# Windowed attention and FFN, six layers: value products with two stationaries per head pair, and another order of the work on five engines

## The reference, cut to what matters

```python
for i in range(6):
    x = attn_layer(shift_tokens(x), Wqkv[i], q_scale[i], k_scale[i], Wo[i]) + x
    x = ffn_layer(shift_tokens(x), ln_g[i], ln_b[i], W1[i], b1[i], W2[i], b2[i]) + x

# attn_layer: 16 heads of 64, windows of 32 tokens
q = l2norm(q) * qs;  k = l2norm(k) * ksc        # then rotary tables with a decay
sim = einsum('bhwie,bhwje->bhwij', bq, bk2) * 8 # 32 queries, 64 keys: window before + own
attn = softmax(where(mask, -max, sim));  out = einsum('bhwij,bhwje->bhwie', attn, bv2)
# ffn_layer: layernorm, x @ W1 + b1, a * gelu(gate), @ W2 + b2 (inner 341)
```

## Time and profile before

| | |
|---|---|
| median of 3 runs | 3135.85 us (3133.73 to 3137.84) |
| profiled execution | 3140.72 us, span 3138.9 us |
| mean granted TensorE clock | 0.989 of full speed (2.4 GHz) |
| PE, PEld busy | 97%, 70% |
| DVE, ACT, POOL busy | 96%, 86%, 81% |

### The profile page before, as it was taken

One profiled execution on the slowest core, in us unless ns is written; L12 is line 12 of the kernel. 1 busy time (PEld: TensorE's weight loads), 2 busy tenths in 40 slices (PEclk: granted clock), 3 DMA queues, 4 the chain that ended last, 5 costly groups with the idle time before them and its releaser, 6 DMA issues.

```text
span 3138.9 us, 168648 instructions
## 1 busy us (share of the span) xinstructions
PE 3047.6 (97%) x71268; PEld 2184.2 (70%) x71268; DVE 3011.6 (96%) x5981; ACT 2692.7 (86%) x5251; POOL 2554.7 (81%) x2803
## 2 busy tenths in 40 slices
PE   6997999999999999999999999999999999999996
PEld 3553777777777777777777777777777777777775
DVE  6997999999999999999999999999999999999995
ACT  5995888888888888888888888888888888888885
POOL 6986888888888888888888888888888888888883
PEclk8998999999999999999999999999999999999998
DMA  3001222223222223222223222223222223222221
GB/s 83 10 10 30 57 52 59 56 52 89 62 52 62 53 52 91 60 54 61 53 56 88 59 58 57 52 60 86 57 62 53 52 62 89 52 62 53 55 60 52
DMA packets 151240, 182.27 MB, mean 58 GB/s; under 512 B 51668, under 2 KB 74258, under 8 KB 151186
## 3 DMA queue, kind: packets, MB, share of 16 engines
q1 hardware_dynamic: 151186, 181.55, 22.3%
HBM read 21.32 MB, written 2.10 MB: 7 GB/s over the span
## 4 chain that ended last, share of the span: by engine, by line
PE 91%; POOL 3%; issue 2%; ACT 2%; DVE 1%; SPq 1%; DMA 0%; POOLq 0%; ACTq 0%; DVEq 0%
PE bank L1518 11%; PE bank L1475 9%; PE bank L1444 8%; PE bank L1546 7%; PE bank L1453 6%; PE bank L1563 5%; PE bank L1408 5%; PE bank L1528 5%; PE bank L1487 5%; PE bank L1554 5%; PE bank L1495 5%; PE bank L1508 5%; PE bank L1501 4%; PE bank L1422 4%; PE bank L1436 2%
## 5 line engine op out<-in xcount | busy, mean ns | idle before, releaser
L1167 DVE TENSOR_REDUCE sm<-sq 128x32 f32<-128x2048 f32 x192 | 437.0, 2276 | 0.0
L1518 PEld LDWEIGHTS bank<-wo,oT 128*128 128x128 f32 x3072 | 372.9, 192 | 91.7 <-issue 90.1
L1518 PE MATMUL bank<-wo,oT 128*128 128x128 f32 x3072 | 374.2, 275 | 0.8 <-ACT gl L839 0.8
L580 POOL TENSOR_TENSOR qk<-qk,rn 128x512 f32<-128x512 f32 x192 | 200.1, 1042 | 213.2 <-DVE rn L1124 213.2
L1475 PEld LDWEIGHTS bank<-PT,vs 64*64 64x64 f32 x18432 | 288.9, 135 | 94.5 <-issue 93.8
L625 POOL TENSOR_TENSOR P<-P,rowsum 128x512 f32<-128x512 f32 x192 | 200.1, 1042 | 154.4 <-DVE rowsum L1202 154.3
L1475 PE MATMUL bank<-PT,vs 64*64 64x32 f32 (+1 forms) x18432 | 311.0, 220 | 4.2 <-issue 4.2
L1546 PEld LDWEIGHTS bank<-cst,qk 32*128 32x128 f32 x12288 | 206.7, 137 | 147.5 <-issue 147.2
L1444 PEld LDWEIGHTS bank<-qkT 64*32 64x32 f32 x24576 | 279.1, 105 | 15.9 <-issue 5.7
L1444 PE MATMUL bank<-qkT 64*32 64x64 f32 x24576 | 282.6, 225 | 4.6 <-issue 4.6
L637 POOL TENSOR_TENSOR qk<-ta,tb 128x512 f32<-128x512 f32 x192 | 245.5, 1279 | 5.8 <-DVE tb L1212 5.8
(11 more groups left out here) (177 smaller groups left out, 9365.5 us busy)
## 6 DMA issues: line engine op xcount, KB each, us to landing
vs<-vt SPq DMA_DIRECT2D x1152, 128.0 KB, 2.4
wqkv<-L_ffn_Wqkv SPq DMA_DIRECT2D x18, 512.0 KB, 3.7
zm<-zm SPq DMA_DIRECT2D x192, 31.8 KB
wo<-L_ffn_Wo SPq DMA_DIRECT2D x6, 512.0 KB, 4.9
z_sb<-x SPq DMA_DIRECT2D x4, 512.0 KB, 6.1
ctxb<-ctx SPq DMA_DIRECT2D x32, 64.0 KB, 1.8
w<-L_ffn_W SPq DMA_DIRECT2D x6, 341.0 KB, 3.2
out<-x_sb SPq DMA_DIRECT2D x7, 256.0 KB, 2.7
```

The lines of the kernel that those rows point to most:

```text
L1167: v_.tensor_reduce(sm[:, :], sq[:, :].rearrange("p (h d) -> p h d", d=DH), AX.X, ALU.add).then_inc(s["d_sumsq"], 1)
L1518: ins = t_.matmul(bank[7][:, 384:512], oT[:, c, :], wo[:, 2 * (c % 4) + c // 4, :], start=c == 0, stop=c == PAIRS - 1)
```

## The change

It has four parts.

1. Value products. The probabilities go to two buffers: PTA with queries 0 to 95 for tokens 0-63, and PTC with queries 64 to 127 for tokens 64-127. For queries 64 to 95, which see tokens 32 to 95, one half of the keys lies in each buffer and the other half is zero there; the copies make the zeros by a scale with a value for each partition (0 or 1). For that the keys and the mask of that window are put in swapped order in the scores. Two stationaries are left, and two DMAs for each half of the heads. The products into PTA and PTC add up in PSUM.
2. Roots. The Newton step moves: ScalarE squares the root (`a_r2`) and forms 3 - x (`a_n2`), GpSimd does the two products (`g_n1`, `g_rn`); VectorE keeps the maximum, now as a reduction over pairs. A factor 0.5 moves into the rotary constants.
3. Order. All engines get another order. TensorE's is now: z transpose, last key projection, value projection, probability transposes of n-3, mask and scores of n-2, transpose of normed z of n-5, value projection, query projection of n+1, gate and FFN of n-5, query projection of n+1, output projection of n-4, q/k transposes of n-1, key projection of n+1, second FFN product of n-5, value products of n-3 (two groups), which are the last thing in the slot. Output projection and FFN run one slot later than before (lags 4 and 5 for 3 and 4).
4. SyncE. The biases of the next layer load at its start, the weights a few steps earlier or later than before. The unrolled start has eight slots for six.

ScalarE's order is now: key square, table load for the gelu, `a_n2` of n-1, vt copy of bank 0, shifted z copy, last quarter to PTC, znT, PTA copy, vt copy of bank 1, third quarter to PTA, query square, gelu, third quarter to PTC, table load, ln, exp of the probabilities, query square, exp of the root, two q/k copies, `a_r2`, key square, two q/k copies, two output copies.

```diff
-                    for j in range(3):
-                        sp.dma_start(vs[rows, par, j, :], vt[32 * j:32 * j + 64, par, r, :]).then_inc(s[f"l_v{par}"], 16)
+                    for j in range(2):
+                        sp.dma_start(vs[rows, par, j, :], vt[64 * j:64 * j + 64, par, r, :]).then_inc(s[f"l_v{par}"], 16)
...
+                    wait(pool, "a_r2", done(u))
+                    g.tensor_tensor(n1[:, :], sc[:, :], n0[:, :], ALU.mult).then_inc(s["g_n1"], 1)
...
+                    wait(pool, "a_n2", done(u))
+                    g.tensor_tensor(rn[:, p, :], rn[:, p, :], n2[:, :], ALU.mult).then_inc(s["g_rn"], 1)
...
+                    a_.activation(n2[:, :], n1[:, :], ACT.Identity, scale=-1.0, bias=three[:, 0:1]).then_inc(s["a_n2"], 1)
...
+                    wait(act, f"l_v{p}", 64 * ((u - 2) // 2) + 64 if isinstance(u, int) else (u >> 1) * 64)
+                    wait(act, "p_v0", done(u))
+                    a_.activation(vt[:, p, 0, :], bank[0][:, :], ACT.Copy).then_inc(s["a_v0"], 1)
...
-                    a_.activation(PT[:, :, 0:64], bank[4][:, :].rearrange("p (h q) -> p h q", h=PAIRS), ACT.Copy).then_inc(s["a_PT0"], 1)
...
+                    a_.activation(PTC[:, :, 32:64], bank[5][:, :].rearrange("p (h q) -> p h q", h=PAIRS)[:, :, 32:64], ACT.Copy).then_inc(s["a_PC1"], 1)
+                    a_.activation(PTA[:, :, 0:64], bank[4][:, :].rearrange("p (h q) -> p h q", h=PAIRS), ACT.Copy).then_inc(s["a_PA0"], 1)
+                    a_.activation(PTA[:, :, 64:96], bank[5][:, :].rearrange("p (h q) -> p h q", h=PAIRS)[:, :, 0:32], ACT.Copy, scale=cst[:, C_HALF:C_HALF + 1]).then_inc(s["a_PA1"], 1)
+                    a_.activation(PTC[:, :, 0:32], bank[5][:, :].rearrange("p (h q) -> p h q", h=PAIRS)[:, :, 0:32], ACT.Copy, scale=cst[:, C_HALF + 1:C_HALF + 2]).then_inc(s["a_PC0"], 1)
...
+                    wait(act, "a_rn", done(u))
+                    a_.activation(n0[:, :], rn[:, p, :], ACT.Square).then_inc(s["a_r2"], 1)
...
-                    v_.scalar_tensor_tensor(sm[:, :], sm[:, :], NORM_MIN2, sm[:, :], ALU.max, ALU.max).then_inc(s["d_nr0"], 1)
+                    v_.tensor_reduce(sc[:, :], sm[:, :, :], AX.X, ALU.max).then_inc(s["d_nr0"], 1)
...
+                    for i in range(4):
+                        for r in range(2):
+                            for e in range(2):
+                                ins = t_.matmul(bank[4 + r][64 * e:64 * e + 64, 128 * i + 0:128 * i + 96],
+                                                vs[kr, p, 0, hc:hc + 64], PTA[kr, 4 * e + i, :],
+                                                start=i == 0, stop=False, skip_group_check=True)
+                    ins.then_inc(s["p_AV0"], 1)
...
+                                ins = t_.matmul(bank[4 + r][64 * e:64 * e + 64, 128 * i + 64:128 * i + 128],
+                                                vs[kr, p, 1, hc:hc + 64], PTC[kr, 4 * e + i, :],
+                                                start=False, stop=True, skip_group_check=True)
+                        if i % 2 == 1:
+                            ins.then_inc(s["p_AV"], 1)
```

More of the change, by code:

```diff
@@ L453, in _ @@
                     shift_v(end + 1, 1)
-                else:
+                if last:
                     store(0, 6)
@@ L458, in _ @@
                     load_o(layer + 1)
+                if not last:
                     shift_v(end + 2, 0)
-                    load_b2(layer + 1)
             store(6, 9)
@@ new lines, in slot @@
+                u, on, p = unit(n, k, -1)
+                if on:
+                    wait(act, "p_qk0", done(u))
+                    wait(act, "d_sumsq", done(u - 1))
+                    a_.activation(sq[:, 0:512], bank[0][:, :], ACT.Square, scale=LN_UP ** 0.5).then_inc(s["a_sq0"], 1)
+                u, on, p = unit(n, k, 5)
+                if on:
+                    wait(act, "p_gate", done(u))
+                    edge(act, u, "d_h", done(u - 1))
+                    for j, (_, m) in enumerate(FCH):
+                        ins = a_.activation(gl[0:m, j, :], bank[7][0:m, 128 * j:128 * j + 128], ACT.Gelu, bias=small[0:m, 5 + j:6 + j])
+                    ins.then_inc(s["a_gelu"], 1)
@@ new lines, in slot @@
+                if on:
+                    wait(act, "p_qk1", done(u))
+                    edge(act, u, "d_sumsq", done(u - 1))
+                    a_.activation(sq[:, 512:1024], bank[1][:, :], ACT.Square, scale=LN_UP ** 0.5).then_inc(s["a_sq1"], 1)
+                u, on, p = unit(n, k, 0)
+                if on:
+                    wait(act, "a_ln", done(u))
+                    edge(act, u, "g_qk0", done(u - 2))
+                    edge(act, u, "g_qk1", done(u - 2))
+                    edge(act, u, "g_qk2", done(u - 2))
+                    edge(act, u, "g_qk3", done(u - 2))
+                    a_.activation(rn[:, p, :], lns[:, :], ACT.Exp, scale=-0.5).then_inc(s["a_rn"], 1)
@@ new lines, in slot @@
+                u, on, p = unit(n, k, 0)
+                if on:
+                    wait(act, "a_rn", done(u))
+                    edge(act, u, "g_n1", done(u - 1))
+                    a_.activation(n0[:, :], rn[:, p, :], ACT.Square).then_inc(s["a_r2"], 1)
+                u, on, p = unit(n, k, -1)
+                if on:
+                    wait(act, "p_qk2", done(u))
+                    edge(act, u, "d_sumsq", done(u - 1))
+                    a_.activation(sq[:, 1024:1536], bank[0][:, :], ACT.Square, scale=LN_UP ** 0.5).then_inc(s["a_sq2"], 1)
@@ L832, in slot @@
                     a_.activation(oT[:, 0:4, :], bank[4][:, :].rearrange("p (h q) -> p h q", h=4), ACT.Copy).then_inc(s["a_AV0"], 1)
-                u, on, p = unit(n, k, 4)
-                if on:
-                    wait(act, "p_gate", done(u))
-                    edge(act, u, "d_h", done(u - 1))
-                    for j, (_, m) in enumerate(FCH):
-                        ins = a_.activation(gl[0:m, j, :], bank[7][0:m, 128 * j:128 * j + 128], ACT.Gelu, bias=small[0:m, 5 + j:6 + j])
-                    ins.then_inc(s["a_gelu"], 1)
@@ L1430, in slot @@
                     edge(pe, u, "a_tr2", done(u))
+                    edge(pe, u, "a_tr3", done(u))
                     pe.nop(nofuse=True)
@@ L1488, in slot @@
                     ins.then_inc(s["p_gate"], 1)
-                u, on, p = unit(n, k, 0)
-                if on:
-                    edge(pe, u, "a_zs", done(u))
-                    edge(pe, u, "d_rot2", done(u))
-                    wait(pe, "l_wv", 16 * layer_of(u) + 16)
-                    t_.matmul(bank[0][:, :], zsT[:, p, :], wv[:, :, 0, :], start=True, stop=True).then_inc(s["p_v0"], 1)
-                u, on, p = unit(n, k, 4)
+                u, on, p = unit(n, k, 5)
                 if on:
@@ L1547, in slot @@
                     ins.then_inc(s["p_tr"], 1)
-                u, on, p = unit(n, k, 4)
+                u, on, p = unit(n, k, -1)
                 if on:
-                    wait(pe, "d_h", done(u))
+                    wait(pe, "d_rot0", done(u))
+                    edge(pe, u, "a_zs", done(u))
+                    wait(pe, "l_wk", 16 * layer_of(u) + 16)
+                    t_.matmul(bank[0][:, :], zsT[:, p, :], wqkv[:, 1024:1536], start=True, stop=True).then_inc(s["p_qk2"], 1)
+                u, on, p = unit(n, k, 5)
+                if on:
+                    edge(pe, u, "d_h", done(u))
                     wait(pe, "l_w2", 32 * layer_of(u) + 32)
```

556 lines of the change are left out of this document (283 added, 273 removed), and 10 rows, old and new, of the table names.

## The result

The changed kernel takes 3192.82 us (median of 4 runs, 3190.42 to 3193.79) against 3135.91 of the kernel before in the same session: 1.0176 times, 95% interval 1.0163 to 1.0189. It is slower, as forecast, but the size is off: +57 us where +27 was forecast. The time lies inside the wide range (3095 to 3220) and outside the forecast's own (3135 to 3180). The span went from 3138.9 to 3191.5 us.

What follows compares the result with a forecast made beforehand. TensorE was taken as the bound, then a 14.77 us loop through the value rows' DMA landing against 14.66 before. 3135.85 + 21 (188 slots x 0.11) + 6 (drain) = 3163 us; own range 3135 to 3180, wide 3095 to 3220.

Steps and rivals of the forecast that it cites:

- Value products at 1.3 us: TensorE's 64 value-product pairs, 32 of 96 and 32 of 64 columns, take 1.3 us a slot against 1.53 before.
- Rival B: Each quadrant loads and streams one after the other: value products stay at 1.5 to 1.6, 3200 to 3219 us; chance 0.20.
- The landing: Value rows' DMAs, issued 0.13 us after the value products, land at 4.25; ScalarE's vt copy waits 0.9 us.
- Rival A: The DMA landing doesn't bind and the slot is TensorE's 14.43 us: 3099 us; chance 0.31.
- ScalarE's row from the copy to the gelu's end: ScalarE's pieces from the vt copy through the gelu take 4.34 us, so the gelu ends at 8.59.
- it starts at 8.64: TensorE's output projection, waiting for the gelu that ends at 8.59, starts at 8.64 us after the z transpose.
- 188 equal slots: About 188 of 192 slots are steady, each losing 0.11 us: +21 us.
- Projection that waited, 1.99: An output projection that waited takes 1.99 us to the next tiled group, 0.1 more, its first load being exposed.
- Drain +6: In the drain the last value products come behind gate, FFN and output products: 6 us, bounds 0 and 14.5.
- TensorE alone 14.43: TensorE's own slot without the landing wait: 13.13 of other work plus 1.3 of value products, 14.43 us.
- Roots at nothing: Moving the root's steps from VectorE to ScalarE and GpSimd buys nothing by itself; their added work is covered.
- Rival C: ScalarE becomes the bound, its scaled and tiny copies taking full duration: 15.2 us a slot, 3243 us; chance 0.05.

Runs made afterwards that it cites:

- e7: e1 with each 96-column value product issued as 64 + 32 columns with the same stationary, 96 pairs for 64; 3200.41 us, ratio 1.0204.
- e1: Changed kernel with ScalarE's last-quarter copy to PTC and half copy to PTA moved ahead of the vt copy that waits for the DMAs; 3137.58 us, ratio 1.001.
- e3: Changed kernel with the four DMAs of value rows moving 256 of 512 columns, so the result isn't the reference's; 3127.47 us, ratio 0.9974.
- e10: Changed kernel with zsT and last-quarter copy ahead of ScalarE's waiting vt copy, register-valued waits of both projections first, TensorE's loop body rotated; 3078.17 us, ratio 0.9816.
- e2: Changed kernel with the two waits ahead of TensorE's output projection swapped: weights' semaphore first, then the gelu's; 3184.52 us, ratio 1.0158.
- e8: e1 with the root's small GpSimd product and ScalarE three-minus step each issued once more into unread buffers; 3157.41 us, ratio 1.0071.
- e11: e10 without the rotation of TensorE's loop body, so the value products end it again; 3093.78 us, ratio 0.9865.
- e9: e1 with TensorE's loop body rotated, so the value products open it and the w2 products end it; 3140.31 us, ratio 1.0011.

## Why the prediction was right or wrong

- *Value products at 1.3 us*: measured 1.29, so 20 ns a pair. The size is right, the way there in part luck: the estimate let the columns set the pace of the 96-column pairs, and in e7 the same columns in more pairs cost 0.32 us more.
- *Rival B, quadrants load and stream in series*: false. 1.29, not 1.5 to 1.6. The strict reading that it made of the rule in the Trainium skill ("TensorE: Matmul & The Clock Gate", "Part 3: Packing small matmuls") would keep the products' time at the old level; the trace disagrees with that reading. The rule itself speaks of equal and different row groups, and no run here sets one against the other.
- *The landing*: issue behind the value products at 0.13, copy 4.12 later by the sum; measured 4.14. Right, and e1 and e3 show that the wait is the loss: moved off, 54 us come back; shortened by 0.34, the slot falls by 0.33. Rival A is false for the change; its price, what TensorE alone allows (3099), is 21 us above what e10 reached.
- *ScalarE's row from the copy to the gelu's end*: 4.34 by the sum, 4.36 measured (1516.04 to 1520.40). Right. The wait was 0.65 to 0.81 for my 0.9.
- ***"it starts at 8.64", 0.05 us behind the gelu's end***: the step that failed. In the loop it started 0.16 to 0.17 behind. The other terms differ by 0.02 at most and cancel, so the slot became 14.89, not 14.77: +0.12, or +23 over 188 slots. The prediction gives no row for its 0.05. It is the lag that the unrolled drain shows (the earlier trace rows and the gelu ahead of it, under e2), and the changed kernel has it in its own drain; it doesn't hold in the loop. e2 shows that the order of two waits moves the loop's lag by 0.03. Why the rest is longer in the loop than in the drain isn't shown.
- *188 equal slots*: the slots outside the window add 0.03 to the mean slot, some 6 us, two thirds of it around the layer changes, which I had priced at nothing.
- *Projection that waited, 1.99*: 1.97. *The groups behind it, 2.84*: 2.84 (1525.38 - 1522.54).
- *Drain +6*: 5.6. *Start -2 to +2*: -3.0.
- *TensorE alone 14.43*: too high by 0.12; e10 has 14.31, of which the value products take 1.29 and all else 13.02, not 13.13. *Roots at nothing*: it fits the changed kernel, whose ScalarE waits 0.65 us for the landing behind the added identity, but no run tested it there; in e1 the queue is tight and the same instructions once more cost 0.10 a slot (e8), though their first price was not measured by itself.
- *VectorE about 87%*: 87.
- Rival C (ScalarE the bound, 15.2 us) is false for the change; what it names was found in e1, in small.

Sum: 27 forecast, +23 for the lag, +6 for the longer slots elsewhere, -3 at the start: 53, the difference of the spans; the other 4 lie between the profiled execution before and its median.

What stays open: why the hand-over takes 0.05 us in the unrolled slots and 0.16 in the loop; why slots are longer around the layer changes and in two of the layers; and whether a third vs buffer, which would let the DMAs be issued before the value products end, is worth more than e10; it does not fit the loop of two slots and wasn't tried.

## What to carry to other kernels

When a transfer's start depends on the last group of a slot and its landing on the first copies of the next, write the loop out as start, landing, queue behind it, hand-over, rest, and add every hand-over between engines from a row of a waiting instruction inside a loop (0.14 to 0.17 us here): the row of the unrolled drain gave 0.05, and in a loop each hundredth counts as often as there are slots. Put the work that needs no landing ahead of the one piece that waits; here the order of five pieces on one engine and of the waits on another was worth the difference between 1.8% slower and 1.3% faster than before (e11), and the loop's turn another 0.5%. And a cure that gives nothing alone is not shown worthless: ScalarE had 0.36 us of idle time in a slot, and each single edit handed the bound to the other engine.

## What the runs showed of the hardware that I had not expected

- A loop body of four slots cost 8.9 us a turn (399 us over 45 turns): 620 transfers of 16 KB on the instruction queue against 37, with TensorE standing 4.0 us at the turn, and the granted clock at 1.2 GHz for 218 of 2600 us behind such pauses.
- The same hand-over from ScalarE to TensorE took 0.05 to 0.06 us in unrolled slots and 0.16 to 0.17 in the loop, and 0.14 in both where its wait came last (the changed kernel and e2).
- The loop's branch on TensorE is hidden behind long matmuls and shows, 0.11 to 0.16 us a turn, behind 64 small ones.
- A matmul group that waits costs its wait and 0.1 us again in the group itself, its first load being exposed: 0.96 for 0.85 in the query projection (e9, e10), 1.97 for 1.87 in the output projection (the changed kernel, e1), as in the earlier trace rows.
- A DMA issue on SyncE's queue took 0.6 us with 128 KB and with 64 (four in 2.39 us in both); halving the 128 KB took 0.34 off the 4.14 from the first issue to the copy that waits.
